# Spectral convolution and normalized residual: the second pass stores 16 map rows, the final pass loads eight of them twice

## The chip, the cores and the metric

The kernel runs on one core of one Trainium2 chip. The metric is the device time of one execution in microseconds (us). Before the change it is 3526.03 us, the median of three runs (3515.51 to 3526.76).

## The reference

The input is x, 16 images of 64 channels of 256 x 256 float32 (16.8 MB an image). Two residual layers follow each other:

```
x = x + spectral(_gn(x)) + bias          # rfft2, 32 x 17 modes mixed within 4 heads of 16 channels, irfft2
m  = mean(xf, axis=0);  mu = m / sqrt(max(m0*m0 - sum(m[1:]**2), EPS))     # xf: tokens x channels of _gn(x)
alpha = max(xf[:,0]*mu[0] - xf[:,1:] @ mu[1:], 1 + EPS);  d = arccosh(alpha)
var  = mean(d*d);  coef = d / sqrt(alpha*alpha - 1)
v  = coef*(xf - alpha*mu);  vo = v - v0/(1+mu0) * (mu with 1 added to mu0)
s  = gamma*vo[:,1:]/(sqrt(var)+EPS) + beta;  t = sqrt(1 + sum(s*s))
x = x + [t, s]
```

`_gn` normalizes pairs of channels of an image. The statistics of the second layer need the whole output of the first, and the variance needs alpha of every token, so x is read three times.

## The kernel before

The kernel is three blocks that follow each other, each with a program for every engine (SP issues most DMAs, GpSimd and ScalarE some). Times are from the start of the profiled span.

**stage_a** (0 to about 1030 us) reads x, computes the 32 x 17 modes, mixes them and stores a spectrum (`spec`) and statistics for every image. The change does not touch it.

**stage_b** (to about 1927 us) is the second pass. It reads an image as 8 tiles of 128 x 4096 (2 MB each, four buffers; SP's `load` of a tile waits until TensorE has finished the tile four before it). Per image:

- GpSimd's `load_modes(b)` asks for the image's spectrum `spt` (two DMAs), `load_dense` for channel 0 (`x0d`).
- VectorE's `combine(b)` contracts the spectrum with the weights of the image (L846 to L853) and raises `v_ready`.
- TensorE's `contract` runs over the 8 tiles; after tile 5 comes `layer_rows(b)` (needs `combine(b)`), after tile 6 `layer_cols(b)`, which needs ScalarE's `copy_z(b)` (L738, L739).
- VectorE's `dense(b)` (L868 to L897), once TensorE has finished the image, makes the maps: `coef` and `beta`, each split into three bf16 parts (high, middle, low), with ScalarE's `distances(b)` (L743 to L751) in between.
- The parts go to DRAM as `maps`, 24 rows of bf16 an image: each part is stored as two rows for the two halves of a channel (s = 0, 1), and each such pair is stored **twice** (index g of `maps_v`). GpSimd's `store_dense` writes the copy g = 0 (L801), along with `bmap` (L802) and `dmap` (L803). ScalarE's `repeat_maps` writes the copy g = 1 (L759, L760), three DMAs for each quarter of the partitions, twelve in all.

The order in each engine's queue is that of its `entry`. On VectorE it is combine(b), dense(b-1), combine(b+1), dense(b). On GpSimd, `entry(b)` is

```
load_modes(b)          # spectrum of b, after combine(b-1)
store_urows(b - 1)
load_dense(b)          # waits for x10 of dense(b-1)
store_dense(b - 1)     # waits for the end of dense(b-1)
```

so the request for the spectrum of b+1 stands behind the stores of image b-1. On ScalarE it is copy_z(b), distances(b), repeat_maps(b), and repeat_maps waits for the end of dense(b), with copy_z(b+1) behind it.

**stage_c** (to the end) is the final pass: 16 tiles of 128 x 2048 an image, four buffers for loads and four for results (`ot`, part of keep_x). For each tile SP issues, in this order, `load_maps` (L1071: 24 rows of 4 KB into every fifth partition of `rt`, then L1073: two DMAs of `bmap`, two partitions each), `load_x` (L1063, 1 MB) and `store` (L1079, 1 MB) of the tile four before the one whose maps are asked for. TensorE multiplies the map rows of `rt` by `lw` (L1160, `p_f` and `p_p`) and the inverse transform by the modes (L1148, `p_u`), VectorE adds and scales (L1270, L1280), ScalarE shifts and squares (L1225, L1232), GpSimd adds (L1322). Rows of `rt` that hold no map are zero. Which row of `lw` meets which part of the split weights is set by masks in `constants()`; six products of parts stand for one float32 product, so a part is needed in one, two or three of them. With 12 rows for each of coef and beta, each product has rows of its own.

Of the kernel before, what the change touches and what calls it, by code (L numbers as in the profile page):

```python
# [19 lines left out]
BF16 = mybir.dt.bfloat16  # L20
ALU = mybir.AluOpType
# [5 lines left out]
HALF = N // 2  # L27
# [7 lines left out]
MAP_AT, MAP_STEP = 4, 5  # L35
MAP_PAIRS = ((0, 2, 4), (1, 3), (5,))


def constants():
# [38 lines left out]
    m = np.zeros((128, 24))  # L78
# [7 lines left out]
    for a, at in enumerate((12, 18)):  # L86
        for part, pairs in enumerate(MAP_PAIRS):
            for pair in pairs:
                for s in range(2):
                    m[MAP_AT + MAP_STEP * (12 * a + 2 * pair + s), at + 2 * part + s] = 1.0  # L90
# [485 lines left out]
def stage_b(nc, ctx, io, B, keep):  # L576
# [7 lines left out]
    maps_v = io["maps"].rearrange("b (q g s) (k j n) -> b g j (s k) q n", q=6, g=2, j=4, n=512)  # L584
# [9 lines left out]
    again_out = sem("again_out")  # L594
# [5 lines left out]
    with ExitStack() as mem:  # L600
# [26 lines left out]
        maps = sb("maps", [128, 6, 512], BF16)  # L627
# [103 lines left out]
        def _(act):  # L731
# [21 lines left out]
            def repeat_maps(b):  # L753

                act.wait_ge(maps_ready, b + 1)
                for j in range(4):
                    at = slice(32 * j, 32 * j + 32)
                    for a in (0, 3):
                        act.dma_start(maps_v[b, 1, j, :, a:a + 2], maps[at, a:a + 2]).then_inc(again_out, 16)  # L759
                    act.dma_start(maps_v[b, 1, j, :, 2::3], maps[at, 0::3]).then_inc(again_out, 16)  # L760

            def entry(b):
                copy_z(b)
                distances(b)
                repeat_maps(b)
# [5 lines left out]
            act.wait_ge(again_out, B * 192)  # L771

        @block.gpsimd
        def _(pool):
# [22 lines left out]
            def store_dense(b):  # L797
                pool.wait_ge(maps_ready, b + 1)
                for j in range(4):
                    at = slice(32 * j, 32 * j + 32)  # L800
                    pool.dma_start(maps_v[b, 0, j], maps[at]).then_inc(maps_out, 16)  # L801
                    pool.dma_start(dense_v(io["bmap"])[b, j], beta[at]).then_inc(beta_out, 16)  # L802
                pool.dma_start(io["dmap"][b], dmap[:].rearrange("p m n -> p (m n)")).then_inc(dmap_out, 16)  # L803

            def entry(b):
                load_modes(b)
                store_urows(b - 1)
                load_dense(b)
                store_dense(b - 1)
# [9 lines left out]
            for b in range(2):  # L819
                P.tensor_copy(awc[:, b, :, 15:47:16], aw[:, b]).then_inc(w_ready[b], 2)  # L820
            load_dense(0)
            pool.wait_ge(uw_ready, 1)
            entry(1)
            with pool.Fori(2, B) as b:
                entry(b)
            store_urows(B - 1)
# [9 lines left out]
        def _(dve):  # L836
# [22 lines left out]
            def dense(b, par):  # L859
# [3 lines left out]
                if not is_at(b, 0):  # L863
                    dve.wait_ge(dmap_out, b * 16)
                    dve.wait_ge(beta_out, b * 64)
                    dve.wait_ge(maps_out, b * 64)
                    dve.wait_ge(again_out, b * 192)
# [17 lines left out]
                both = ((coef, 0, w1), (beta, 3, w2))  # L885
# [10 lines left out]
                ch.inc(V.tensor_tensor(maps[:, 2], w1[:], maps[:, 1], ALU.subtract))  # L896
                V.tensor_tensor(maps[:, 5], w2[:], maps[:, 4], ALU.subtract).then_inc(maps_ready, 1)  # L897
# [108 lines left out]
PER_B = 15  # L1006
# [8 lines left out]
def stage_c(nc, ctx, io, B, keep):  # L1015
# [21 lines left out]
    with ExitStack() as mem:  # L1037
# [20 lines left out]
        def _(sp):  # L1058
# [6 lines left out]
            def load_maps(b, t):  # L1065
# [5 lines left out]
                sp.dma_start(r[MAP_AT:MAP_AT + 24 * MAP_STEP:MAP_STEP], maps_v[b, t]).then_inc(r_in[t % NB], 16)  # L1071
# [57 lines left out]
        def _(pe):  # L1129
# [7 lines left out]
            def first_layer(b, t, n):  # L1137
                g = b * GR + 2 * t + n
                if n == 0:
                    pe.wait_ge(r_in[t % NB], b * (48 * T // NB) + 48 * (t // NB) + 48)  # L1140
# [207 lines left out]
def program(nc, args, B):  # L1348
    io = dict(args)
    dram = lambda n, s, d=FP32: nc.dram_tensor(n, s, d, kind="Internal").ap()  # L1350
    with ExitStack() as ctx:
# [4 lines left out]
        io["maps"] = dram("maps", (B, 24, HALF), BF16)  # L1356
# [52 lines left out]
```

## Time and profile before

| | before |
|---|---|
| median of 3 runs | 3526.03 us (3515.51 to 3526.76) |
| the profiled execution: time, span | 3532.95 us, 3531.4 us |
| busy: TensorE, VectorE, ScalarE, GpSimd | 82%, 75%, 61%, 43% of the span |
| moved by DMA | 1211.86 MB, 343 GB/s on average |
| DMA packets | 289224 |
| of them on ScalarE's queue (q10), 192 issues | 15360, 12.60 MB |
| granted TensorE clock, mean | 0.91 |

The three stages have different limits, so the totals say little; the stages have to be read one by one. The share of DMA time in a stretch is a mean over 16 DMA engines: at 1.00 all sixteen are busy all the time. "Idle before <-releaser" is the time in which an engine had nothing to run, and what ended it.

### The profile page before, as it was taken

How to read it: one execution, taken by the hardware profiler on the slowest of the kernel's cores; microseconds unless marked ns; L12 is line 12 of the kernel's file. 1: busy time of each engine (PE TensorE's matmuls, PEld its weight loads, DVE VectorE, ACT ScalarE, POOL GpSimd, SP SyncE). 2: the span in 40 equal slices, each digit the busy share in tenths (PEclk: the TensorE clock that was granted, in tenths of full speed). 3: DMA queues.
4: the chain of work that ended last, by engine and by line, in shares of the span. 5: the costliest groups of instructions: out<-in, count | busy, mean ns of one | idle time of the engine just before them, and what ended most of it. 6: DMA issues, size and time to landing. Idle time of an engine off the chain costs nothing. (4 is left out here: it accounts for less than half of the span.)

```text
span 3531.4 us, 69910 instructions
## 1 busy us (share of the span) xinstructions
PE 2885.8 (82%) x26018; PEld 1417.7 (40%) x26018; DVE 2643.3 (75%) x2594; ACT 2159.8 (61%) x2994; POOL 1521.1 (43%) x895
## 2 busy tenths in 40 slices
PE   6999999999725776676673998888889888888887
PEld 3555555555501222222222544444444444444443
DVE  0788888888878544644643898888888888888888
ACT  6988888888600101101101788877778778777777
POOL 0101010101111112112111787777778777777777
PEclk9999999999858978888886999999999999999999
DMA  9888787879629999999995899999999999999998
GB/s 376 299 306 301 290 312 279 324 275 327 263 82 357 361 391 398 398 378 378 385 378 185 310 376 391 377 369 385 381 379 373 372 375 370 372 371 379 378 383 341
DMA packets 289224, 1211.86 MB, mean 343 GB/s; under 512 B 32305, under 2 KB 45302, under 8 KB 206710
## 3 DMA queue, kind: packets, MB, share of 16 engines
q1 hardware_dynamic: 258518, 1152.93, 85.1%
q0 software_dynamic: 15136, 43.40, 3.8%
q10 hardware_dynamic: 15360, 12.60, 1.2%
q8 instruction: 148, 2.42, 0.3%
q14 instruction: 62, 0.51, 0.0%
HBM read 884.40 MB, written 324.32 MB: 342 GB/s over the span
## 5 line engine op out<-in xcount | busy, mean ns | idle before, releaser
L1322 POOL TENSOR_TENSOR keep_x<-keep_x,c_pp 128x1024 f32<-128x1024 f32 x512 | 1215.3, 2375 | 360.1 <-DVE keep_x L1280 358.9
L1270 DVE SCALAR_TENSOR_TENSOR keep_x<-keep_x,keep_k,c_p_u 128x1024 f32<-128x1024 f32 x512 | 653.8, 1277 | 126.5 <-PE c_p_u L1148 100.1
L1280 DVE SCALAR_TENSOR_TENSOR keep_x<-c_p_f,keep_k,keep_x 128x1024 f32<-128x1024 f32 x512 | 657.2, 1284 | 107.5 <-DMA out<-keep_x 57.3
L1225 ACT ACTIVATE c_pp<-c_p_p,keep_cols 128x1024 f32<-128x1024 f32 x512 | 571.2, 1116 | 254.8 <-PE c_p_p L1160 253.5
L1148 PE MATMUL c_p_u<-keep_mv,c_zc 64*128 64x256 f32 x4096 | 594.1, 409 | 75.7 <-DVE keep_x L1270 74.6
L1232 ACT ACTIVATE c_sq<-keep_x,keep_cols 128x1024 f32<-128x1024 f32 x512 | 584.8, 1142 | 61.0 <-DVE keep_x L1270 60.7
L336 ACT ACTIVATE a_junk<-keep_x 128x1024 bf16<-128x1024 f32 x512 | 537.9, 1055 | 27.2 <-DMA keep_x<-in_x 19.9
L255 PE MATMUL a_p_rows<-keep_x,a_dft_h 128*64 128x512 f32 x2048 | 514.9, 646 | 37.1 <-DMA a_bias_t<-in_bias 18.7
L1148 PEld LDWEIGHTS c_p_u<-keep_mv,c_zc 64*128 64x128 f32 x4096 | 360.6, 190 | 358.5 <-issue 218.2
L1160 PE MATMUL c_p_f<-c_rt,keep_lw 64*128 64x512 bf16 x1024 | 313.2, 386 | 103.7 <-DVE keep_x L1280 91.1
L522 POOL TENSOR_TENSOR a_sm<-a_sm 128x8 f32<-128x8 f32 x16 | 26.8, 1674 | 824.8 <-DVE a_sm L463 824.8
L685 PE MATMUL b_p_al<-keep_x,b_awc 128*32 128x512 f32 x2048 | 288.9, 640 | 89.7 <-DMA keep_x<-in_x 64.2
L743 ACT ACTIVATE b_dn<-b_dn,b_minus 128x512 f32<-128x512 f32 x16 | 11.6, 724 | 500.5 <-DVE b_dn L871 500.5
L1160 PE MATMUL c_p_p<-c_rt,keep_lw 64*128 64x512 bf16 x1024 | 316.4, 390 | 0.0
L403 DVE TENSOR_REDUCE a_y<-a_prod 128x68 f32<-128x2176 f32 x128 | 309.9, 2421 | 5.6
L400 DVE TENSOR_TENSOR a_prod<-a_wm,a_xh 128x2176 f32<-128x2176 f32 x128 | 309.3, 2416 | 0.3
L1174 PE MATMUL c_p_t<-c_sq,c_hw 128*32 128x512 f32 x2048 | 288.5, 637 | 1.3 <-ACT c_sq L1232 1.3
L846 DVE TENSOR_TENSOR b_prod<-b_spt,b_arow 64x2176 f32<-64x2176 f32 x16 | 38.7, 2417 | 333.9 <-DMA b_spt<-spec 333.8
L685 PE MATMUL b_p_ls<-keep_x,b_awc 128*32 128x512 f32 x2048 | 280.3, 622 | 0.0
L1134 PEld LDWEIGHTS c_p_z<-keep_idft,keep_ys 128*37 128x37 f32 x7936 | 232.5, 114 | 105.6 <-issue 105.6
L1134 PE MATMUL c_p_z<-keep_idft,keep_ys 128*37 128x64 f32 x7936 | 271.6, 221 | 0.0
L255 PEld LDWEIGHTS a_p_rows<-keep_x,a_dft_h 128*64 128x64 f32 x2048 | 136.1, 146 | 308.2 <-issue 187.2
(205 smaller groups left out, 3007.2 us busy)
## 6 DMA issues: line engine op xcount, KB each, us to landing
keep_x<-in_x SPq DMA_DIRECT2D x512, 1024.0 KB, 12.3
keep_x<-in_x SPq DMA_DIRECT2D x128, 2048.0 KB, 16.4
out<-keep_x SPq DMA_DIRECT2D x256, 1024.0 KB, 16.2
c_rt<-maps SPq DMA_DIRECT2D x256, 96.0 KB
maps<-b_maps ACTq DMA_DIRECT2D x192, 64.0 KB, 13.1
maps<-b_maps POOLq DMA_DIRECT2D x64, 192.0 KB, 9.2
dmap<-b_dmap POOLq DMA_DIRECT2D x16, 768.0 KB, 13.8
c_dmap<-dmap SPq DMA_DIRECT2D x16, 768.0 KB, 16.3
```

The source lines that it names most:

```text
L255: last = nc.tensor.matmul(p_rows[i][64 * t:64 * t + 64, :], dft_h[:, j], xt[q % NX][:, t::2, i, j * W:(j + 1) * W], start=(j == 0), stop=( ...
L336: nc.scalar.activation(junk[h % 2][:].rearrange("p (i w) -> p i w", i=2), xt[q % NX][:, h], ACT.Square, accum_out=sq[:, q, h:h + 1]).then_ ...
L403: ch.step(V.tensor_reduce(y[:, 2 * q:2 * q + 2, 0:M2].rearrange("p o (a k) -> p o a k", a=2), prod[:].rearrange("p o a (k n) -> p o a k n" ...
L685: last = nc.tensor.matmul(out[32 * j:32 * j + 32, :], awc[:, par, kind, 15 - k:47 - k], xt[t % NX][:, at:at + 512], start=(k == 0), stop=F ...
L1134: last = nc.tensor.matmul(p_z[64 * at:64 * at + YS, 64 * c:64 * c + 64], ys[:, 8 * part + c], idft[:, chunk, at], start=True, stop=True)
L1148: last = nc.tensor.matmul(p_u[:, 512 * at + W * r:512 * at + W * r + W], zc[t // CH][64 * at:64 * at + 64, i], mv[t % NB][64 * at:64 * at ...
L1160: last = nc.tensor.matmul(p[:, 512 * k:512 * k + 512], keep["lw"][at:at + 64, b].rearrange("p c s -> p (c s)"), rt[t % NB][at:at + 64, c:c ...
L1225: S.activation(pp[n][:], p_p[:], ACT.Identity, bias=keep["cols"][:, b, 1:2]).then_inc(pp_done, 1)
L1232: S.activation(sq[t % 2][:, 1024 * n:1024 * n + 1024], xt[t % NB][:, 1024 * n:1024 * n + 1024], ACT.Square, scale=keep["cols"][:, b, 0:1]) ...
L1270: V.scalar_tensor_tensor(out=u, in0=u, scalar=kc, in1=p_u[:], op0=ALU.mult, op1=ALU.add).then_inc(u_done, 1)
L1280: V.scalar_tensor_tensor(out=ot[t % NB][:, at], in0=p_f[:], scalar=kinv, in1=xt[t % NB][:, at], op0=ALU.add, op1=ALU.mult).then_inc(f_done, 1)
L1322: P.tensor_tensor(o, o, pp[n][:], ALU.add).then_inc(o_done, 1)
```

## The change

Each part is stored once. `maps` becomes 16 rows an image: eight that the final pass needs twice or once in an order fixed by `MAP_ROWS`. VectorE writes eight bf16 maps in place of six: 0 to 3 as before (coef high and middle, beta high and middle), 4 and 6 are copies of 0 and 2 (one instruction over both), 5 and 7 are the low parts. GpSimd's DMA L801 of 32 x 6 x 512 becomes one of 32 x 8 x 512. `repeat_maps` goes from ScalarE, with its wait and its twelve DMAs an image, and so does VectorE's wait for them.

In the final pass `load_maps` issues two DMAs for the maps in place of one: rows 0 to 7 of the 16, each read into two partitions (16 partitions, every eighth from 2), and rows 8 to 15 (8 partitions, every sixteenth from 6). Together they fill 24 partitions as before.

GpSimd's `entry(b)` asks for the spectrum of b+1 first, so the request stands behind combine(b) and in front of load_dense(b) and store_dense(b-1).

```diff
-MAP_AT, MAP_STEP = 4, 5
-MAP_PAIRS = ((0, 2, 4), (1, 3), (5,))
+TWICE_AT, ONCE_AT = 2, 6
+MAP_ROWS = (((0, 0), (0, 1), (1, 1)), ((2, 0), (2, 1)), ((1, 0),))
...
-        maps = sb("maps", [128, 6, 512], BF16)
+        maps = sb("maps", [128, 8, 512], BF16)
...
-            def repeat_maps(b):
-
-                act.wait_ge(maps_ready, b + 1)
-                for j in range(4):
-                    at = slice(32 * j, 32 * j + 32)
-                    for a in (0, 3):
-                        act.dma_start(maps_v[b, 1, j, :, a:a + 2], maps[at, a:a + 2]).then_inc(again_out, 16)
-                    act.dma_start(maps_v[b, 1, j, :, 2::3], maps[at, 0::3]).then_inc(again_out, 16)
-
             def entry(b):
                 copy_z(b)
                 distances(b)
-                repeat_maps(b)
...
-                    pool.dma_start(maps_v[b, 0, j], maps[at]).then_inc(maps_out, 16)
+                    pool.dma_start(maps_v[b, j], maps[at]).then_inc(maps_out, 16)
...
-            def entry(b):
-                load_modes(b)
-                store_urows(b - 1)
+            def entry(b, last=False):
+                if not last:
+                    load_modes(b + 1)
+                store_urows(b)
                 load_dense(b)
                 store_dense(b - 1)
...
+            load_modes(1)
             load_dense(0)
             pool.wait_ge(uw_ready, 1)
+            store_urows(0)
             entry(1)
...
-                    dve.wait_ge(again_out, b * 192)
...
-                both = ((coef, 0, w1), (beta, 3, w2))
+                both = ((coef, 0, w1), (beta, 2, w2))
...
-                ch.inc(V.tensor_tensor(maps[:, 2], w1[:], maps[:, 1], ALU.subtract))
-                V.tensor_tensor(maps[:, 5], w2[:], maps[:, 4], ALU.subtract).then_inc(maps_ready, 1)
+                ch.inc(V.tensor_copy(maps[:, 4::2], maps[:, 0:4:2]))
+                ch.inc(V.tensor_tensor(maps[:, 5], w1[:], maps[:, 1], ALU.subtract))
+                V.tensor_tensor(maps[:, 7], w2[:], maps[:, 3], ALU.subtract).then_inc(maps_ready, 1)
...
-                sp.dma_start(r[MAP_AT:MAP_AT + 24 * MAP_STEP:MAP_STEP], maps_v[b, t]).then_inc(r_in[t % NB], 16)
+                sp.dma_start(r[TWICE_AT::8], maps_v[b, t, 0:8].unsqueeze(1).to_broadcast((8, 2, TC))).then_inc(r_in[t % NB], 16)
+                sp.dma_start(r[ONCE_AT::16], maps_v[b, t, 8:16]).then_inc(r_in[t % NB], 16)
...
-        io["maps"] = dram("maps", (B, 24, HALF), BF16)
+        io["maps"] = dram("maps", (B, 16, HALF), BF16)
```

GpSimd's queue in the second pass, before the change: `entry(1)`, which is written out ahead of the loop (L781 is load_modes, L788 store_urows, L795 load_dense, L801 to L803 store_dense).

```order
L781 DMA b_spt<-spec 32x4x592 x2
L788 DMA spec<-b_uw 8x16x3
L795 DMA b_dn<-in_x 32x512 x4
L801 DMA maps<-b_maps 32x6x512
L802 DMA bmap<-b_dn 32x512
...
L803 DMA dmap<-b_dmap 128x1536
```

The same place after the change: the first two rows of spectrum, dense input and urows are those that stand ahead of `entry(1)`, which begins with the second L770 (L770 is load_modes, L777 store_urows, L784 load_dense, L790 to L792 store_dense).

```order
L770 DMA b_spt<-spec 32x4x592 x2
L784 DMA b_dn<-in_x 32x512 x4
L777 DMA spec<-b_uw 8x16x3
L770 DMA b_spt<-spec 32x4x592 x2
L777 DMA spec<-b_uw 8x16x3
L784 DMA b_dn<-in_x 32x512 x4
L790 DMA maps<-b_maps 32x8x512
L791 DMA bmap<-b_dn 32x512
...
L792 DMA dmap<-b_dmap 128x1536
```

The spectrum requests moved one image ahead, and the map stores are four DMAs of eight maps in place of six.

SP's queue in the final pass, before: the maps, bmap, x and the store of one tile.

```order
L1071 DMA c_rt<-maps 24x2048
L1073 DMA keep_mv<-bmap 2x2x512 x2
L1063 DMA keep_x<-in_x 128x2048
L1079 DMA out<-keep_x 128x2048
L1071 DMA c_rt<-maps 24x2048
```

And after:

```order
L1063 DMA c_rt<-maps 16x1x2048
L1064 DMA c_rt<-maps 8x2048
L1066 DMA keep_mv<-bmap 2x2x512 x2
L1055 DMA keep_x<-in_x 128x2048
L1072 DMA out<-keep_x 128x2048
```

One DMA of 24 rows became one of 16 partitions and one of 8; the rest of the tile's order is the same.

## Rows read from the trace of the kernel before

**Rows 1.** Windows: PE, PEld, DVE, ACT, POOL busy (instructions), granted clock, DMA share, GB/s.

```profile
1131.00:1161.00 30.00, 18.51 (x112) 7.29 (x116) 16.71 (x11) 3.15 (x5) 5.62 (x11) 0.64 0.60 184
1160.00:1869.00 709.00, 500.98 (x3736) 163.47 (x3728) 369.93 (x350) 83.36 (x123) 117.94 (x212) 0.85 1.00 387
...
2110.00:3480.00 1370.00, 1211.42 (x14128) 612.43 (x14124) 1174.64 (x942) 1090.33 (x1121) 1066.75 (x458) 0.97 0.97 376
```

**Rows 2.** Timeline of VectorE, one image of the second pass: start, us, line.

```profile
1414.93 2.42 DVE L846 TENSOR_TENSOR b_prod<-b_spt,b_arow 64x2176 f32<-64x2176 f32 x1 [22.56 <-DMA b_spt<-spec]
...
1429.26 0.75 DVE L868 TENSOR_SCALAR b_dn<-b_p_al,b_ac 128x512 f32<-128x512 f32 x1 [0.67 <-PE b_p_ls L685]
...
1443.12 0.69 DVE L897 TENSOR_TENSOR b_maps<-b_dn,b_maps 128x512 bf16<-128x512 f32 x1
...
1466.85 2.42 DVE L846 TENSOR_TENSOR b_prod<-b_spt,b_arow 64x2176 f32<-64x2176 f32 x1 [22.63 <-DMA b_spt<-spec]
```

**Rows 3.** Timeline of GpSimd, the same image.

```profile
1444.54 0.59 POOL L801 DMA_DIRECT2D maps<-b_maps  x1 [10.95 <-DVE b_maps L897]
...
1450.48 1.20 POOL L781 DMA_DIRECT2D b_spt<-spec  x2 [0.44 <-issue]
```

**Rows 4.** Timeline of ScalarE, then of TensorE, one image earlier.

```profile
1392.14 0.80 ACTq L759 DMA_DIRECT2D maps<-b_maps  x2
...
1398.21 0.59 ACT L738 ACTIVATE b_zs<-b_p_z 34x512 f32<-34x512 f32 x1 [12.97 <-issue]
...
1399.12 2.07 PE L704 MATMUL b_p_y<-keep_idft_w,b_zs 34*128 34x256 f32 x4 [12.10 <-ACT b_zs L739]
```

**Rows 5.** Timeline of TensorE, the second image of the second pass.

```profile
1142.49 2.07 PE L704 MATMUL b_p_y<-keep_idft_w,b_zs 34*128 34x256 f32 x4 [26.36 <-ACT b_zs L739]
```

**Rows 6.** Timeline of TensorE in the last image of the second pass, then of VectorE.

```profile
1852.46 1.07 PE L685 MATMUL b_p_al<-keep_x,b_awc 128*32 128x512 f32 x8 [1.24 <-DMA keep_x<-in_x]
1857.35 1.06 PE L685 MATMUL b_p_al<-keep_x,b_awc 128*32 128x512 f32 x8 [1.25 <-DMA keep_x<-in_x]
1860.92 1.05 PE L695 MATMUL b_p_z<-keep_idft_h,b_vm 128*34 128x256 f32 x4
...
1879.08 2.07 PE L704 MATMUL b_p_y<-keep_idft_w,b_zs 34*128 34x256 f32 x4 [13.10 <-ACT b_zs L739]
...
1886.20 1.93 PE L685 MATMUL b_p_ls<-keep_x,b_awc 128*32 128x512 f32 x8
...
1893.08 0.75 DVE L868 TENSOR_SCALAR b_dn<-b_p_al,b_ac 128x512 f32<-128x512 f32 x1 [21.42 <-DMA maps<-b_maps]
```

**Rows 7.** DMA queues (packets, MB, share of 16 engines) and issues, 1160 to 1880 us.

```profile
q0 software_dynamic: 11256, 35.80, 14.6%
q10 hardware_dynamic: 12686, 10.41, 4.8%
...
maps<-b_maps ACTq DMA_DIRECT2D x168, 64.0 KB, 13.7
maps<-b_maps POOLq DMA_DIRECT2D x56, 192.0 KB, 9.5
```

**Rows 8.** DMA, 1932.4 to 1933.9 us: one tile's maps and bmap.

```profile
DMA packets 48, 0.11 MB, mean 77 GB/s; under 512 B 16, under 2 KB 16, under 8 KB 48
...
q1 hardware_dynamic: 48, 0.11, 26.1%
```

**Rows 9.** Timelines of the final pass: VectorE's first tile; SP, one tile.

```profile
1952.18 1.28 DVE L1270 SCALAR_TENSOR_TENSOR keep_x<-keep_x,keep_k,c_p_u 128x1024 f32<-128x1024 f32 x1 [21.36 <-PE c_p_u L1148]
...
2262.08 0.75 SPq L1071 DMA_DIRECT2D c_rt<-maps  x1
...
2266.44 0.37 SPq L1079 DMA_DIRECT2D out<-keep_x  x1
```

**Rows 10.** Waits of VectorE, 2110 to 3480 us: total, times, longest.

```profile
DVE keep_x L1280 <- DMA out<-keep_x: 56.4, 87, 1.5
DVE keep_x L1270 <- DMA keep_x<-in_x: 21.5, 29, 1.4
```

**Rows 11.** Timeline of GpSimd and ScalarE: the last stores of the second pass.

```profile
1912.17 0.57 POOL L803 DMA_DIRECT2D dmap<-b_dmap  x1
...
1919.07 0.32 ACTq L760 DMA_DIRECT2D maps<-b_maps  x1
```

More of the change, by code:

```diff
@@ L86, in constants @@
     for a, at in enumerate((12, 18)):
-        for part, pairs in enumerate(MAP_PAIRS):
-            for pair in pairs:
+        for part, rows in enumerate(MAP_ROWS):
+            for kind, n in rows:
                 for s in range(2):
-                    m[MAP_AT + MAP_STEP * (12 * a + 2 * pair + s), at + 2 * part + s] = 1.0
+                    row = ONCE_AT + 16 * (4 * a + 2 * n + s) if kind == 1 else TWICE_AT + 8 * (2 * (4 * a + 2 * n + s) + kind // 2)
+                    m[row, at + 2 * part + s] = 1.0
     c["misc"] = m
@@ L583, in stage_b @@
     dense_v = lambda a: a.rearrange("b s (k j n) -> b j (s k) n", j=4, n=512)
-    maps_v = io["maps"].rearrange("b (q g s) (k j n) -> b g j (s k) q n", q=6, g=2, j=4, n=512)
+    maps_v = io["maps"].rearrange("b (q s) (k j n) -> b j (s k) q n", s=2, j=4, n=512)
     x_in, bc_in = keep["bx_in"], keep["bc_in"]
@@ L593, in stage_b @@
     e_ready, maps_ready, maps_out, beta_out, dmap_out = sem("e_ready"), sem("maps_ready"), sem("maps_out"), sem("beta_out"), sem("dmap_out")
-    again_out = sem("again_out")
     var_in, var_mm, std_ready = sem("var_in"), sem("var_mm"), sem("std_ready")
@@ L770, in _ @@
                 entry(b)
-            act.wait_ge(again_out, B * 192)
         @block.gpsimd
@@ L820, in _ @@
                 P.tensor_copy(awc[:, b, :, 15:47:16], aw[:, b]).then_inc(w_ready[b], 2)
+            load_modes(1)
             load_dense(0)
             pool.wait_ge(uw_ready, 1)
+            store_urows(0)
             entry(1)
-            with pool.Fori(2, B) as b:
+            with pool.Fori(2, B - 1) as b:
                 entry(b)
-            store_urows(B - 1)
+            entry(B - 1, last=True)
             store_dense(B - 1)
@@ L1003, in _ @@
             ch.step(V.tensor_scalar(keep["k"][:, 2:3], keep["k"][:, 0:1], 2.0, None, ALU.mult))
-PER_B = 15
+PER_B = 16
 def load_modes_0(sp, keep, spec, half):
@@ L1139, in first_layer @@
                 if n == 0:
-                    pe.wait_ge(r_in[t % NB], b * (48 * T // NB) + 48 * (t // NB) + 48)
+                    pe.wait_ge(r_in[t % NB], b * (64 * T // NB) + 64 * (t // NB) + 64)
                     if t % CH == 0:
```

## The prediction

> **What bounds the kernel now.** I read the windows by stage first, then the timelines of one image of the second pass, engine by engine, and last the DMA queues. The first pass (to about 1030 us) is not touched, so it drops out.
>
> In the second pass the sixteen DMA engines are full: share 1.00 at 387 GB/s from 1160 to 1869 us [rows 1]. Next to that stands a loop of waits of the same length. VectorE ends an image's maps at 1443.8 (L897) and then waits 22.63 us for the next spectrum [rows 2]. GpSimd issues the stores first, from 1444.54, and asks for the spectrum at 1450.48 [rows 3]; it is there at 1466.85. Combine (1414.93 to about 1428.6) and dense (1429.26 to 1443.8) follow. From L846 to L846 that is 1466.85 - 1414.93 = 51.9 us, all of it accounted for: 6 us of GpSimd's issues, 16.4 us of landing, 13.7 us of combine, 15.2 us of dense, and small waits.
>
> The second thing to see is TensorE. ScalarE copies the rows that TensorE needs (L738) only after its own stores, which wait for the end of dense: stores from 1392.14, the copy at 1398.21, TensorE at 1399.12 after 12.10 us of waiting [rows 4]. In mid-stage the four tile buffers cover this, since the DMA share is still 1.00. At two places they don't. In the second image the same wait is 26.36 us [rows 5], and the DMA share between 1131 and 1161 us falls to 0.60 [rows 1]: 0.40 x 30 = 12 us of DMA lost. In the last image nothing is left to hide it: tiles reach TensorE 4.9 us apart (1852.46, 1857.35), the wait is 13.10 us, and the matmuls after it run at the lower clock (1.93 us for eight, against 1.06 before it), so that dense starts at 1893.08 [rows 6].
>
> In the final pass the DMA share is 0.97, TensorE is busy 1211 and VectorE 1175 of 1370 us [rows 1], and VectorE waits in turn for stored buffers (56.4 us) and loads (21.5 us) [rows 10]. I take DMA as its limit, and a few of the sixteen engines, not their mean. One tile's maps and bmap are 24 packets of 4 KB and eight of 2 KB, 32 in all, plus 16 small ones that close a DMA on each engine it uses [rows 8]; 16 = 12 + 2 + 2, so 24 rows go over 12 engines with two rows each, and each bmap DMA over two. If all start from the same engine, the busiest carries per tile 65.5 KB of loads, 65.5 of stores, 8.2 of maps, 8.2 of bmap and 6.5 for its part of dmap, spectrum and channel 0 (1.65 MB an image over 16 engines and 16 tiles): 154 KB. A tile takes (3531 - 1952)/256 = 6.17 us [rows 9], so this engine moves 25.0 GB/s. An engine of the second pass at share 1.00 moves 387/16 = 24.2 GB/s. The mean engine of the final pass moves 376/16 = 23.5. So the busiest is already at full pace.
>
> **The second pass, part by part.** *Twelve DMAs of ScalarE go.* q10 is 4.8% of 720 us, 34.6 us of all sixteen engines for 168 issues, 14 images [rows 7]: 2.47 us an image. *GpSimd's stores grow* from 12 to 16 rows, 0.262 MB an image. q0 takes 14.6% of 720 us for 35.80 MB [rows 7], 2.94 us per MB, so +0.77 us. Net 1.70 us an image; for the 15 images whose stores fall under the loads, -25.5 us. *ScalarE's wait goes*, and with it the loss at the start: -12 us. *The spectrum is asked for after combine instead of behind the stores.* This opens the loop: during dense (15.2 us) the 16.4 us of landing are nearly over, so VectorE's 22.6 us shrink to one or two. By itself this gives nothing, as the DMA engines are at 1.00; it only keeps the loop from being the limit at 51.9 once the DMA work is 50.2. What is late next is the load of x. TensorE has 3.57 us of work a tile (1857.35 to 1860.92 [rows 6]) against some 6.2, so it is not. One thing moves the other way: dense of the last image but one now ends before the last tile has been read, where its stores came after it. These are 2.10 MB of q0: 2.94 x 2.10 = +6.2 us. The last tile thus lands 25.5 + 12 - 6.2 = 31 us sooner.
>
> *The end of the pass.* The last tile came two tiles after the one at 1857.35, by 1868 to 1869. Without the 13.10 us, and with the clock up, dense could start 3.6 us later, at 1872.6, against 1893.08: -20 us. Its own stores end no later: GpSimd's last issue was at 1912.17, ScalarE's at 1919.07 [rows 11]; I count -1. Second pass: -31 - 20 - 1 = -52 us. The bounds: -35, if the start's loss stays as waits of another kind and late stores cost what they save; -65, if the engines, freed of ScalarE's 1 KB packets, also run the x loads better.
>
> *Costed at nothing:* VectorE's added copy of two maps. All of dense is 15.2 us and VectorE idles 22.6 an image [rows 2]; were that cover gone, it would be under 1 us an image. load_dense(0) now waits behind combine(0), long before dense(0). In the final pass SP issues one DMA more a tile: an issue takes 0.75 us, and SP's tile runs from 2262.08 to 2266.4 of some 6 [rows 9].
>
> **The final pass.** The bytes and the 24 filled partitions are the same, but one DMA of 24 rows becomes one of 8 rows read twice and one of 8. I take the twice-read DMA to be cut where both of its sides can be cut, at the 8 rows in memory, as 24 rows were cut into 12 x 2 [rows 8]. Then eight engines carry 2 + 1 = 3 rows where twelve carried 2, and the busiest gets one 4 KB row more per tile. At 25.0 GB/s that is 4.1/25.0 = 0.164 us, times 256 tiles: **+42 us**. The low end is 0: the busiest engine carries two rows as before, or the mean decides. For the high end the isolated tile of rows 8 serves: 26.1% of 16 engines over 1.5 us is 6.3 us for 115 KB, 0.22 us for 4.1 KB, so +57. I stay near the low price, since in the full queue a row is one packet among long ones.
>
> The Trainium skill (DMA: Bandwidth & Descriptors, "Why a DMA increments its semaphore by 16 and not by 1") speaks against this change: a DMA issued from SP runs on the largest number of engines up to 16 that divides the slowest dimension of both patterns, the lowest-numbered ones. The 12 and 2 of this trace agree; for 16 partitions against 8 rows it gives 8, beginning with the same engines as bmap, and thus the sum above. The same page's rules for kernel authors say that DMAs of all issuers share the same 16 engines, so that leaving ScalarE's queue is no loss; the rows show shares by queue, not that.
>
> **The sum.** -52 + 42 = -10 us. The profiled execution took 3532.95, so its like would take 3523. It stood 7 us above the median of the three runs; from that median the forecast is **3516 us**. The bound between a change and none is 0.3%, 10.6 us, so the forecast sits just inside it: the two halves are each five times larger than their difference.
>
> **The rivals.**
>
> 1. *The final pass loses nothing.* The DMA of 16 partitions uses 16 engines, so that the busiest has 1 + 1 rows, or the mean share of 0.97 is what counts, and that does not change. For it: VectorE's DMA waits are only 78 us of 1370 [rows 10], and the busy shares of TensorE and VectorE are close behind [rows 1]. Against it: 0.97 is what is left if most engines idle while a few are full; if 154 KB is the pace and the mean is 145, 0.94 would be expected. Then 3526 - 52 = 3474 us. Chance 0.17.
> 2. *The third row costs more than its bytes* (the other side). The second maps DMA is short and lands rows in the middle of long loads on the same eight engines; at the price of rows 8, 0.22 us a tile, the final pass loses 57, and with 38 us of gain in the second pass the kernel ends at 3545 us, slower. It decides from 52/256 = 0.20 us a tile upwards. For it: three DMAs on the same first engines. Against: full-queue rates are near the low price. Chance 0.16.
> 3. *The second pass gains only bytes.* Its DMA engines are full now, and the start's 12 us come back as a wait for loads, or the spectrum (which is asked for only after combine, late in the image) stays exposed. Then 25.5 - 6.2 + 20 = 39 us against 42: 3529 us. Chance 0.15.
>
> **How the numbers follow.** The main case has 0.52 and by itself the range 3505 to 3527; it gives faster and same in about equal parts (0.27, 0.24, 0.01). Rival 1 is faster, rival 3 the same, rival 2 slower, with small parts over the edges: faster 0.45, same 0.38, slower 0.17. The range reaches nearly to rival 1's time and takes in most of rival 2's: 3478 to 3541 us.
>
> **What would show it.** Right: VectorE's wait for b_spt is a few us an image; TensorE's wait for b_zs is gone; the distance of L846 to L846 is near 50 us; dense of the last image starts about 50 us sooner; the share from 1131 on shows no hole; the final pass, from its first L1148 to the end, is some 40 us longer, its DMA share falls below 0.97, and a tile's maps close with 8 + 8 + 2 + 2 = 20 small packets. Wrong: 28 small packets with an unchanged final pass (rival 1); a final pass longer by 55 (rival 2); an image still at 52 us (rival 3). If the share stays at 0.97 while the pass grows, my busiest engine is not the cause.

## The result and the profile after

| | before | after |
|---|---|---|
| median | 3523.59 us (16 runs, 3512.08 to 3548.53, and one of 10876.57) | 3546.37 us (16 runs, 3529.41 to 3562.65) |
| ratio | | 1.0062, 95% interval 1.0042 to 1.0082 |
| profiled execution: time, span | 3532.95, 3531.4 us | 3538.95, 3537.4 us |
| granted TensorE clock, mean | 0.910 | 0.924 |

The kernel became slower by 22 us, where 10 us faster was forecast. The profile of before lay 9 us above its median and that of after lies 7 us below its own, so that two spans side by side hide most of the difference. Times between kernels are therefore taken from ratios to the kernel before (on the same chip each time) and turned into microseconds with 3524.

The page of the profile after: its span, its packets and its two large queues. The third queue of before (q10, ScalarE's) has no line any more.

```profile
span 3537.4 us, 69577 instructions
...
DMA packets 275915, 1203.49 MB, mean 340 GB/s; under 512 B 30257, under 2 KB 30966, under 8 KB 193398
...
q1 hardware_dynamic: 259542, 1152.93, 86.5%
q0 software_dynamic: 16160, 47.60, 3.8%
```

The windows of after, which answer to [rows 1] (the last one lies 50 us earlier, as the final pass does):

```profile
1131.00:1161.00 30.00, 23.31 (x184) 5.66 (x176) 12.86 (x5) 0.00 (x0) 6.12 (x11) 0.90 1.01 412
1160.00:1820.00 660.00, 479.51 (x3498) 142.35 (x3498) 380.34 (x373) 83.54 (x123) 118.54 (x211) 0.91 1.01 384
2060.00:3430.00 1370.00, 1181.14 (x13698) 600.04 (x13695) 1132.01 (x908) 1054.84 (x1083) 1030.39 (x442) 0.96 0.96 365
```

The hole at the start of the second pass is filled (DMA share 0.60 before, 1.01 now), and the pass stays full. In the final pass the share fell from 0.97 to 0.96 and the rate from 376 to 365 GB/s: the same work moves more slowly, by engines that are hardly less busy.

The second pass of after, where [rows 2 to 4] and [rows 6] were. VectorE (end of dense, then combine), one image:

```profile
1405.76 0.68 DVE L889 TENSOR_TENSOR b_maps<-b_dn,b_maps 128x512 bf16<-128x512 f32 x1
1406.67 0.17 DVE L895 COPY b_awc<-b_aw 128x4 f32 x1 [0.23 <-DVE b_maps L889]
1407.19 2.42 DVE L838 TENSOR_TENSOR b_prod<-b_spt,b_arow 64x2176 f32<-64x2176 f32 x1 [0.34 <-issue]
```

GpSimd's request, and TensorE behind ScalarE's copy:

```profile
1390.92 1.20 POOL L770 DMA_DIRECT2D b_spt<-spec  x2 [24.82 <-DVE b_vm L845]
```

```profile
1383.26 1.13 PE L704 MATMUL b_p_y<-keep_idft_w,b_zs 34*128 34x256 f32 x4
```

The request goes out as soon as combine ends, the spectrum is there when VectorE wants it (0.34 us in place of 22.63), and the 12 us of TensorE have gone too. From the first L838 of an image to that of the next, images 3 to 14 take 48.9 us on average, where the same images took 53.7 before (the 51.9 of [rows 2] is one of them). The last image, TensorE's sixth tile and VectorE's dense, and then VectorE's first tile of the final pass:

```profile
1831.79 1.07 PE L685 MATMUL b_p_al<-keep_x,b_awc 128*32 128x512 f32 x8 [2.29 <-DMA keep_x<-in_x]
```

```profile
1847.85 0.75 DVE L859 TENSOR_SCALAR b_dn<-b_p_al,b_ac 128x512 f32<-128x512 f32 x1 [29.82 <-PE b_p_ls L685]
```

```profile
1903.16 1.28 DVE L1263 SCALAR_TENSOR_TENSOR keep_x<-keep_x,keep_k,c_p_u 128x1024 f32<-128x1024 f32 x1 [21.36 <-PE c_p_u L1141]
```

The sixth tile came 25.6 us sooner (1857.35 before), dense 45.2 us, the final pass 49.0 us [rows 6, 9]. So the second pass did what it should. The final pass, from that instruction to the end of the span, grew from 3531.4 - 1952.18 = 1579.2 to 3537.4 - 1903.16 = 1634.2 us: 55 us. VectorE's waits in it, against [rows 10]:

```profile
DVE keep_x L1273 <- DMA out<-keep_x: 76.5, 113, 2.0
DVE keep_x L1263 <- DMA keep_x<-in_x: 45.1, 38, 3.5
```

Both grew, by 20 and 24 us: loads and stores come later. SP's queue from 1882 to 1892 us holds the maps and bmap of four tiles and nothing else:

```profile
DMA packets 209, 0.48 MB, mean 48 GB/s; under 512 B 80, under 2 KB 80, under 8 KB 208
...
q1 hardware_dynamic: 208, 0.46, 15.7%
```

80 small packets are 20 a tile, 8 + 8 + 2 + 2. The DMA that reads eight rows twice runs on eight engines, which is what the rule of the Trainium skill gives for 16 partitions against 8 rows (DMA: Bandwidth & Descriptors, "Why a DMA increments its semaphore by 16 and not by 1"). The trace agrees with the number of engines by these packets, and 24 rows over twelve engines had closed with 16. It does not say which engines they are.

### The profile page after: what moved, and what is told of

The parts are those of the page before. It is cut to its first block and busy times, and to the rows that moved or that the text cites. A ratio compares the mean times of both kernels' runs of the same rounds, so it can differ in the third digit from the quotient of the medians.

```text
span 3537.4 us, 69577 instructions
## 1 busy us (share of the span) xinstructions
PE 2903.2 (82%) x26018; PEld 1410.9 (40%) x26018; DVE 2647.2 (75%) x2610; ACT 2160.4 (61%) x2994; POOL 1523.9 (43%) x895
## 5 line engine op out<-in xcount | busy, mean ns | idle before, releaser
L1141 PE MATMUL c_p_u<-keep_mv,c_zc 64*128 64x256 f32 x4096 | 603.4, 414 | 99.4 <-DVE keep_x L1263 93.7
L685 PE MATMUL b_p_al<-keep_x,b_awc 128*32 128x512 f32 x2048 | 305.6, 671 | 225.2 <-DMA keep_x<-in_x 199.6
L685 PE MATMUL b_p_ls<-keep_x,b_awc 128*32 128x512 f32 x2048 | 296.9, 653 | 0.0
L738 ACT ACTIVATE b_zs<-b_p_z 34x512 f32<-34x512 f32 x16 | 9.4, 588 | 461.2 <-PE b_p_zl L696 461.2
L281 PE MATMUL a_p_cols<-a_dft_w,a_cols 128*128 128x34 f32 x2048 | 243.9, 275 | 0.0
## 6 DMA issues: line engine op xcount, KB each, us to landing
b_spt<-spec POOLq DMA_DIRECT2D x32, 296.0 KB, 13.7
```

The lines of the kernel that those rows point to most:

```text
L685: last = nc.tensor.matmul(out[32 * j:32 * j + 32, :], awc[:, par, kind, 15 - k:47 - k], xt[t % NX][:, at:at + 512], start=(k == 0), stop=F ...
L1141: last = nc.tensor.matmul(p_u[:, 512 * at + W * r:512 * at + W * r + W], zc[t // CH][64 * at:64 * at + 64, i], mv[t % NB][64 * at:64 * at ...
```

## The experiments

**The theories.** *A*: the final pass goes at the pace of its busiest DMA engines. They carried four 4 KB rows of maps and bmap a tile before (2 rows of maps, 1 of each bmap DMA) and carry five now (2 + 1 of maps, 1 + 1 of bmap), if all these DMAs begin with the same engines. The rivals: the added DMA of each tile, the double read or the new partitions cost, wherever the rows fall (*B*); the early request for the spectrum made the gain of the second pass (*C*); the number of DMAs, the bytes or the mean load of the engines decide, not where the rows fall (*D*, and *B* in the last run). *F* and *G* are about the second pass alone and come up with experiment 10. The paragraph ahead of each result is what was expected before the run. The diffs show the main lines; the ends `.then_inc(...)` and the counts and masks that follow from an edit are left out.

**1. The same loads on sixteen and eight engines.** The 16 stored rows are read once by one DMA and eight of them again by the other, so that nothing is read twice within a DMA. In this kernel some rows meet the other half of the weights: the same work, another output.

```diff
-                sp.dma_start(r[TWICE_AT::8], maps_v[b, t, 0:8].unsqueeze(1).to_broadcast((8, 2, TC)))
-                sp.dma_start(r[ONCE_AT::16], maps_v[b, t, 8:16])
+                sp.dma_start(r[TWICE_AT::8], maps_v[b, t])
+                sp.dma_start(r[ONCE_AT::16], maps_v[b, t, 0:8])
```

> The changed kernel, but in the final pass all 16 map rows are loaded by one DMA into 16 partitions (every eighth from 2) and the eight that are needed twice by a second one (every sixteenth from 6); the masks follow. Same bytes, same number of DMAs, same 24 partitions; only the rows per DMA engine differ: 1 + 1 on eight engines and 1 on the other eight, where the change has 2 + 1 on eight. Theory A (the busiest DMA engine sets the pace of the final pass): the final pass falls back to its length before the change, some 55 us shorter than after it, and the kernel takes about 3475 to 3495 us. Rival B (the second DMA per tile with its issue on SP, the double read or the new partitions cost the time): it stays near 3546 us.

Measured: 3485.69 us, ratio 0.9892 (0.9871 to 0.9912), final pass 1584.2 us. 60 us faster than the change with the same number of DMAs, rows and bytes, and the same second pass. So neither the added DMA nor the partitions nor the bytes explain these 60 us. Where the rows fall is different, and no DMA reads a row twice; experiments 8 and 11 take these two apart.

**2. The kernel before, with its 24 rows cut into 16 and 8.**

```diff
-                sp.dma_start(r[MAP_AT:MAP_AT + 24 * MAP_STEP:MAP_STEP], maps_v[b, t])
+                for lo, n in ((0, 16), (16, 8)):
+                    at = MAP_AT + lo * MAP_STEP
+                    sp.dma_start(r[at:at + n * MAP_STEP:MAP_STEP], maps_v[b, t, lo:lo + n])
```

> The kernel before, with its 24 rows loaded by two DMAs, of 16 and of 8 rows, into the same partitions. One DMA issue more per tile; at most two rows on any engine, as before. Theory A: the same as before within 0.3% (3513 to 3535 us), closing packets 16 + 8 + 2 + 2 = 28 a tile. Rival B (one more DMA per tile is what costs): 40 to 60 us slower, about 3570 us.

Measured: 3534.52 us (12 runs), ratio 1.0039 (1.0014 to 1.0064), final pass 1591.8 us. The busiest engine has four rows as before; one more DMA a tile costs 14 us (5 to 23), not the 40 to 60 of B. This was a term that the prediction had at nothing.

**3. The change without GpSimd's new order.**

```diff
-            def entry(b, last=False):
-                if not last:
-                    load_modes(b + 1)
-                store_urows(b)
+            def entry(b):
+                load_modes(b)
+                store_urows(b - 1)
```

> The changed kernel with GpSimd's old order: the next spectrum is asked for behind the stores of the dense part. Theory A, by which the second pass gains by bytes, by the DMA hole at its start and by the wait at its end: the loop of waits is back (VectorE waits some 22 us an image for the spectrum), but it is as long as the DMA work, so this is 0 to 20 us slower than the change. Rival C (the early request made the gain of the second pass): 40 us or more slower than the change, about 3590 us.

Measured: 3751.78 us, ratio 1.0657 (1.0630 to 1.0685). A expected 0 to 20 us more than the change, C 40 us or more and a kernel of about 3590 us; it is 210 us. The final pass is as long as in the change (1630.9 us); the second pass ends 216 us later. VectorE's combine of two images, and GpSimd's request between them:

```profile
1428.86 2.42 DVE L835 TENSOR_TENSOR b_prod<-b_spt,b_arow 64x2176 f32<-64x2176 f32 x1 [39.59 <-DMA b_spt<-spec]
...
1496.17 2.42 DVE L835 TENSOR_TENSOR b_prod<-b_spt,b_arow 64x2176 f32<-64x2176 f32 x1 [37.90 <-DMA b_spt<-spec]
```

```profile
1464.53 1.21 POOL L770 DMA_DIRECT2D b_spt<-spec  x2 [0.44 <-issue]
```

An image takes 67.3 us in place of 51.9, and the spectrum lands 31.6 us after its request in place of 16.4. TensorE, and the DMA share of the stretch before the request and of that behind it:

```profile
1442.51 1.91 PE L695 MATMUL b_p_z<-keep_idft_h,b_vm 128*34 128x256 f32 x4 [28.27 <-DVE b_vm L842]
```

```profile
1430.00:1460.00 30.00, 15.93 (x90) 5.75 (x94) 26.84 (x27) 6.02 (x9) 3.29 (x7) 0.65 0.39 147
1464.00:1496.00 32.00, 18.32 (x153) 4.58 (x144) 0.00 (x0) 0.00 (x0) 2.11 (x4) 0.88 1.02 377
```

TensorE stands with all its buffers full while it waits for combine, and the DMA engines idle (0.39). Then it runs through its tiles, the loads of x go out one after another, and the request for the spectrum joins them.

**4. The kernel before, with GpSimd's new order alone.** The reverse of that diff.

> The kernel before with GpSimd's new order alone; ScalarE still stores its 12 rows an image. Theory A: ScalarE's wait in front of its copy for TensorE stays whenever dense ends late, but dense now starts as soon as TensorE has finished an image, so the copy comes early and TensorE's waits of 12 us an image shrink as well; the DMA work is unchanged at some 51 us an image; gain 5 to 35 us, 3490 to 3520 us. Rival C: the whole 50 us of the second pass, 3475 us.

Measured: 3514.14 us (12 runs), ratio 0.9971 (0.9952 to 0.9989): 10 us faster (4 to 17), as A had it and far from C's 3475. With ScalarE's wait in place the order matters little.

**5. Two DMAs of twelve rows.** Two of the eight stored maps are copies, so the high parts of coef and beta are in fact stored twice and only the other parts once. The stored rows are put in another order (the copies are now maps 0 and 6), so that two overlapping DMAs, rows 0 to 11 and rows 4 to 15, fill the 24 partitions.

```diff
-                sp.dma_start(r[TWICE_AT::8], maps_v[b, t, 0:8].unsqueeze(1).to_broadcast((8, 2, TC)))
-                sp.dma_start(r[ONCE_AT::16], maps_v[b, t, 8:16])
+                for at, lo in ((FIRST_AT, 0), (SECOND_AT, 4)):
+                    sp.dma_start(r[at:at + 12 * ROW_STEP - ROW_STEP + 1:ROW_STEP], maps_v[b, t, lo:lo + 12])
```

> The changed kernel with the 16 stored rows in another order and two loads of 12 rows each that overlap (rows 0 to 11 and 4 to 15), so each of twelve DMA engines gets one row from each: two rows on the busiest, as before the change, and the reference's result. Theory A (the busiest engine sets the pace): as the 16 + 8 form, 3480 to 3495 us, some 60 us under the change. Rival B (the new partitions or the double read cost the time, and the 16 + 8 form was quick for another reason): above 3520 us.

Measured: 3489.99 us, ratio 0.9910 (0.9884 to 0.9936), final pass 1590.7 us. It leaves nothing out and is faster than both kernels: 54 us less than the change (42 to 66), 32 us less than before. VectorE's two waits fall back to those of [rows 10]:

```profile
DVE keep_x L1273 <- DMA out<-keep_x: 56.0, 90, 1.8
DVE keep_x L1263 <- DMA keep_x<-in_x: 25.1, 27, 1.6
```

**6. That kernel without bmap**, which it loads for the first four tiles only; the term of beta in the other tiles is left out.

```diff
-                    sp.dma_start(m[64 * at + M2:64 * at + M2 + 2]..., bmap_v[b, t, at])
+                    if b == 0 and t < NB:
+                        sp.dma_start(m[64 * at + M2:64 * at + M2 + 2]..., bmap_v[b, t, at])
```

> The same, but bmap is loaded for the first four tiles only, and each later tile uses what lies in its buffer; the beta term of the other tiles is left out of the right place, so this measures the cost of those two small DMAs of a tile, 8 KB on each of two engines. Theory A: these two engines lose 8 KB of about 154 a tile and no longer stand out against the ten others with two map rows: 50 to 85 us faster than the form with bmap, about 3420 us, until compute (5.54 us a tile where no DMA is waited for) takes over. Rival D (the mean of the engines or HBM is the limit): 16 KB of 2.3 MB a tile, 0.7% of 1600 us, at most 12 us faster.

Measured: 3418.66 us, ratio 0.9708 (0.9685 to 0.9732), 71 us less. By D these 16 KB of a tile are worth 12 us at most. The two DMAs are 28 us of the 71 by the price of experiment 2, the rest falls to two rows on two engines. Two rows at 54 us (the step from experiment 5 to the change) and two DMAs would be some 135 us; but ten other engines now have two rows as well, and VectorE's waits for stores, 56 us in experiment 5, are 3.6. What limits this kernel was not looked for further.

**7. The change with one more DMA of two rows**, one more row on two engines.

```diff
+                sp.dma_start(spare[t % NB][:], maps_v[b, t, 0:2]).then_inc(r_in[t % NB], 16)
```

> The changed kernel with one more DMA per tile, of two rows of 4 KB into a spare tile that nobody reads: one row more on two engines. Theory A: the busiest engines carry four rows, +42 us for the row and about +12 for the DMA itself (the 16 + 8 form of the kernel before cost 11): 3590 to 3610 us. Rival D: 8 KB of 2.3 MB, +5 us, plus 12 for the DMA: 3560 us.

Measured: 3628.65 us, ratio 1.0313 (1.0281 to 1.0345), 88 us more than the change. Less 14 us for a DMA that is 74 us for a row. It is above A's 3590 to 3610 and further from D's 3560: the price of a row was too low here as well.

**8. The kernel before, its 24 rows in three DMAs of eight**, so that each of eight engines has three.

```diff
-                sp.dma_start(r[MAP_AT:MAP_AT + 24 * MAP_STEP:MAP_STEP], maps_v[b, t])
+                for lo in (0, 8, 16):
+                    at = MAP_AT + lo * MAP_STEP
+                    sp.dma_start(r[at:at + 8 * MAP_STEP:MAP_STEP], maps_v[b, t, lo:lo + 8])
```

> The kernel before with its 24 rows loaded by three DMAs of eight rows into the same partitions: three rows on eight engines, no row read twice. Theory A: +42 us for the third row and about +11 for each of the two added DMAs: 3580 to 3595 us. Rival B (double read or partitions): only the two DMAs, 3540 to 3550 us.

Measured: 3602.80 us, ratio 1.0239 (1.0206 to 1.0271), 70 us more than experiment 2: 14 us for a DMA and 56 us for a row. It is again a little above A's 3580 to 3595, and B's 3540 to 3550 is out. So the price holds in a kernel with the second pass of before, with no row read twice.

**9. bmap by four DMAs of one partition.** Meant to spread bmap over many engines, on the kernel of experiment 5; bmap lies in DRAM such that each of these rows is 4 KB in one piece.

```diff
-                    sp.dma_start(m[64 * at + M2:64 * at + M2 + 2]..., bmap_v[b, t, at])
+                    for s in range(2):
+                        p = 64 * at + M2 + s
+                        sp.dma_start(m[p:p + 1].rearrange("p (e n) -> p e n", e=PIECES), bmap_v[b, t, at, s:s + 1])
```

> The kernel with two DMAs of 12 rows, with bmap laid out in DRAM so that each row of a tile is 4 KB in one piece, and loaded by four DMAs of one partition each in place of two DMAs of two partitions. The bytes are the same; two DMAs a tile are added; a DMA of one partition can be cut along its row over many engines. Theory A (the first engines, which carry the most rows, set the pace of the final pass): each of the two bmap DMAs with two partitions put one row on each of two engines, so two rows a tile leave the busiest; at 0.22 us a row that is up to 0.44 x 256 = 113 us less, against two added DMAs at 0.045 us each a tile (+23 us) and more, smaller packets: 3400 to 3470 us against 3490. Theory D (the number of DMAs and of packets sets the pace, not where the rows fall): 3513 us or more.

Measured: 3626.84 us, ratio 1.0314 (1.0298 to 1.0330), 142 us more than experiment 5. By the words on record that speaks for D, but their premise, that such a DMA is cut over many engines, was wrong. SP's queue with the loads of four tiles and nothing else, of experiment 5 (1880 to 1892 us) and then of this one (1881 to 1894 us):

```profile
DMA packets 241, 0.48 MB, mean 40 GB/s; under 512 B 112, under 2 KB 112, under 8 KB 240
...
c_rt<-maps SPq DMA_DIRECT2D x8, 48.0 KB
keep_mv<-bmap SPq DMA_DIRECT2D x8, 8.0 KB
```

```profile
DMA packets 225, 0.48 MB, mean 37 GB/s; under 512 B 112, under 2 KB 112, under 8 KB 224
...
c_rt<-maps SPq DMA_DIRECT2D x8, 48.0 KB
keep_mv<-bmap SPq DMA_DIRECT2D x16, 4.0 KB
```

Both close with 112 small packets, 28 a tile: 12 + 12 + 2 + 2 there and 12 + 12 + 4 x 1 here. Each of the four DMAs ran on a single engine, in one 4 KB packet. If that is the same engine each time, which the trace does not show, the busiest now has 1 + 1 + 4 = 6 rows in place of 4. Two rows at 54 us and two DMAs at 14 are 136 us; 142 were measured. D would have to explain 142 us by two DMAs without a byte more, ten times what one DMA cost in experiment 2. This run was explained after its result, so it supports A less than experiments 5, 8 and 11 do.

**10. Experiment 3 with ScalarE's wait put back**, with no DMA behind it.

```diff
             def entry(b):
                 copy_z(b)
                 distances(b)
+                act.wait_ge(maps_ready, b + 1)
```

> The changed kernel with GpSimd's order of before, as in the run that took 3751.8 us, and ScalarE waits after distances(b) until dense(b) has ended, as repeat_maps made it wait before, but with no DMA behind the wait. Theory F (ScalarE's wait held TensorE's buffers back while the spectrum was on its way, so that no deep queue of x loads stood in front of it; with the wait gone the spectrum lands 15 us later, and that is in the loop): the wait brings the period of an image back from 67 us to about 50 to 52, the spectrum lands in 16 to 20 us, and the time is 3540 to 3600 us. Theory G (what is lost without the new order has another cause, such as the larger stores of GpSimd ahead of the request): the time stays above 3700 us.

Measured: 3562.41 us (4 runs), ratio 1.0130 (1.0112 to 1.0147). One added wait makes the kernel 186 us faster. GpSimd asks at 1444.64 and VectorE goes on at 1458.33:

```profile
1444.64 1.20 POOL L771 DMA_DIRECT2D b_spt<-spec  x2 [0.44 <-issue]
```

```profile
1458.33 2.42 DVE L836 TENSOR_TENSOR b_prod<-b_spt,b_arow 64x2176 f32<-64x2176 f32 x1 [19.96 <-DMA b_spt<-spec]
```

13.7 us in place of 31.6. SP's queue, which holds the loads of x, while the spectrum was under way, in experiment 3 (1464.5 to 1496.2 us) and here (1444.6 to 1458.4 us):

```profile
q1 hardware_dynamic: 649, 9.58, 81.4%
```

```profile
q1 hardware_dynamic: 121, 1.72, 43.3%
```

9.58 MB of x shared the engines with it there and 1.72 MB here, while GpSimd's own queue moved about the same (2.34 and 2.52 MB). An image takes 51.4 us on average (images 3 to 14), against 66.4 in experiment 3. Theory F holds and G is out: the wait that looked like pure loss had held TensorE's buffers back while the spectrum was under way.

**11. Every row read twice.** The rows in the order of experiment 5, one DMA into 32 partitions; eight of them meet weights of zero.

```diff
+                sp.dma_start(r[ROW_AT::ROW_STEP], maps_v[b, t].unsqueeze(1).to_broadcast((16, 2, TC)))
```

> The changed kernel with the 16 stored rows in the order of the kernel with two DMAs of 12 rows, and in the final pass one DMA that reads each of the 16 rows into two partitions (32 partitions, every fourth from 2; the eight that no product needs meet weights of zero). Per tile eight rows (32.8 KB) more are moved than in the changed kernel, by three DMAs in place of four. Theory A (the final pass goes at the pace of its busiest engines): the maps DMA is cut over sixteen engines with two rows each, the busiest has 2 + 2 rows and three DMAs, as in the kernel before; the added rows fall on engines that have time. Against the kernel with two DMAs of 12 rows one DMA a tile goes (-11 us): 3475 to 3485 us, a final pass of about 1579 us, a ratio near 0.988. Theory B (the mean load of the sixteen engines sets the pace): 32.8 KB at 387 GB/s is 0.085 us a tile, +22 us on the changed kernel's rows, so 3500 to 3515 us and a final pass of 1600 us or more.

Measured: 3489.25 us, ratio 0.9904 (0.9882 to 0.9926), final pass 3486.1 - 1901.31 = 1584.8 us. Its windows, against the last row of after above:

```profile
2060.00:3430.00 1370.00, 1213.34 (x14106) 614.49 (x14108) 1172.36 (x941) 1087.96 (x1119) 1065.34 (x456) 0.97 0.99 381
```

It moves 32.8 KB a tile more than the change and takes 56 us less. The share rose to 0.99, so the added bytes are not free: A's 3475 to 3485 was a little low, D's 3500 and more too high (B in the text on record). The DMA that it saves against experiment 5 and the bytes that it adds about cancel. Here every row is read twice within one DMA, and the pass is short: the double read is not what costs in the change.

**The runs in one table** (rows of 4 KB a tile on the busiest engine, DMAs a tile for maps and bmap):

| kernel | rows | DMAs | final pass, profile | ratio |
|---|---|---|---|---|
| before | 4 | 3 | 1579.2 | 1 |
| 4: before, new order | 4 | 3 | 1578.8 | 0.9971 |
| 2: before, 16 + 8 | 4 | 4 | 1591.8 | 1.0039 |
| 8: before, 3 x 8 | 5 | 5 | 1658.9 | 1.0239 |
| 11: all twice | 4 | 3 | 1584.8 | 0.9904 |
| 5: two of twelve | 4 | 4 | 1590.7 | 0.9910 |
| 6: without bmap | 2 | 2 | 1516.4 | 0.9708 |
| 1: sixteen and eight | 4 | 4 | 1584.2 | 0.9892 |
| **after** | 5 | 4 | 1634.2 | 1.0062 |
| 3: after, old order | 5 | 4 | 1630.9 | 1.0657 |
| 10: after, old order, ScalarE waits | 5 | 4 | 1635.0 | 1.0130 |
| 7: after, one row more | 6 | 5 | 1730.8 | 1.0313 |
| 9: bmap by single rows | 6 | 6 | 1719.4 | 1.0314 |

The final pass follows the first two columns, in both families, whatever the second pass was. Experiments 7 and 9 alone stand the other way round, by 11 us of their single profiles; their ratios are equal.

**What the packets say.** The runs show that the placing of a tile's rows sets the time. They do not show the engines beyond the first ones standing idle for it, as one would expect if these alone held the pass up. The stretch from 2060 to 3430 us of before, of experiment 8 and of experiment 7:

```profile
2060.00:3430.00 1370.00, 1215.46 (x14224) 614.76 (x14224) 1176.15 (x942) 1096.56 (x1128) 1071.35 (x459) 0.97 0.98 376
2060.00:3430.00 1370.00, 1166.51 (x13566) 591.59 (x13564) 1120.43 (x900) 1045.59 (x1075) 1022.58 (x438) 0.97 0.98 359
2060.00:3430.00 1370.00, 1126.83 (x12936) 568.47 (x12940) 1072.79 (x862) 998.11 (x1023) 973.44 (x417) 0.95 0.96 345
```

In experiment 8 the DMA share is that of before, at 359 in place of 376 GB/s. Added up over the packets of the final pass in the traces, as a mean of the sixteen engines:

| kernel | final pass | in packets | idle | mean of an 8 KB packet |
|---|---|---|---|---|
| 6 | 1516.4 us | 1489.7 us | 26.7 us | 329 ns |
| before | 1579.2 us | 1523.6 us | 55.6 us | 334 ns |
| 5 | 1590.7 us | 1534.8 us | 56.0 us | 337 ns |
| 2 | 1591.8 us | 1536.1 us | 55.7 us | 337 ns |
| after | 1634.2 us | 1550.3 us | 83.9 us | 341 ns |
| 8 | 1658.9 us | 1595.2 us | 63.7 us | 351 ns |
| 7 | 1730.8 us | 1632.1 us | 98.7 us | 359 ns |

The 8 KB packets are the rows of x and of the result, some 64,900 in each kernel, and their median is 309 ns in every one. Of the 55 us between before and after, half is idle time and half is longer packets; from experiment 2 to 8, and from after to 7, it is nearly all longer packets. Why the packets of x take longer when the first engines carry one row more is not shown by any run.

## Why the prediction was wrong

Three differences lead from before to after: experiment 2, experiment 5 and the change.

| step | forecast | measured, from ratios |
|---|---|---|
| one more DMA a tile (2 against before) | 0 | +14 (5 to 23) |
| second pass (5 against 2) | -52 | -45 (-58 to -33) |
| third row on eight engines (after against 5) | +42 | +54 (42 to 66) |
| sum | -10 | +22 (rounded once) |

- **The step that failed** is the price of the final pass, "4.1/25.0 = 0.164 us, times 256 tiles: +42 us", with the added DMA of each tile "costed at nothing". Together they measured 14 + 54 = 68 us, 0.27 us a tile. The placing was right: the twice-read DMA runs on eight engines (20 small packets a tile), so that they have three rows, and the first engines are shared with bmap as far as experiment 6 shows it. The row is 0.21 us a tile here and 0.22 in experiment 8, the high end that came from the isolated tile [rows 8], and 0.29 in experiment 7. The argument for the low end, that in a full queue a row is one packet among long ones, was not borne out for the pass, though it was for the packet: a 4 KB packet took 159 ns (median of 2110 to 3400 us) before and after, which is the 0.164 of the sum. What the sum lacks is what the row does to the packets around it. On the added DMA the prediction looked only at SP's time to issue it; whether its 14 us lie there or on the engines is open.
- **The second pass** came within its bounds. From the sixth tile of the last image on: -25.6 us where -31 was forecast, then -19.6 to dense (forecast -20) and -3.8 to the final pass (forecast -1); these are differences of two profiles, of which that of before was slower than its median (see below). The start's hole is gone, as forecast. Experiment 10 splits it: against the change it still has the old order and ScalarE's wait, and is 24 us slower (15 to 33). If the parts add up, the remaining 21 us of 45 are ScalarE's DMAs less GpSimd's larger stores, where the sum had 25.5, or 19 with the 6.2 of the last stores.
- **"By itself this gives nothing"**, of the early request, was wrong in a way that no rival had. Alone in the kernel before it gives 10 us; but without ScalarE's wait it is what keeps the loop of spectrum, combine and TensorE short, and the kernel without it takes 210 us more. "What is late next is the load of x" was right of the change and wrong of the change without the new order, where the spectrum is late (experiment 3).
- **Rival 2** is what happened, by a slightly other sum: 57 against 38 us there, 68 against 45 here. Its deciding point was 52/256 = 0.20 us a tile; the final pass lost 0.27. Rival 1 is out (20 small packets, a longer final pass). Rival 3 is out by its signs: the start has no hole (share 1.01), VectorE's wait for the spectrum is gone, and an image takes 48.9 us. Its gain of 39 us by itself lies within the measured 33 to 58.
- **The last sign** of the prediction reads against it: "If the share stays at 0.97 while the pass grows, my busiest engine is not the cause." The share went to 0.96, where the prediction's way of counting (145 KB on the mean engine, 158 on the busiest) would have it at 0.92, and in experiment 8 it did not fall at all. Experiments 1, 5, 8 and 11 show that the rows on the busiest engines decide; that they do so by leaving the other engines idle is only half true of the change and hardly of experiment 8.
- The base was off as well. The profile of before was slower than its median: its final pass began at 1952.2 us, while those of experiments 2 and 8, with the same first two passes, began at 1929.1 and 1942.8. The seven profiles with the second pass of after began it between 1897.9 and 1903.2.

## What to carry to other kernels

Where DMA bounds a stage, count rows and DMAs on the busiest engine, not the mean: the small closing packets of an isolated tile tell how many engines each DMA takes, and a row a tile moved off the busiest engines was worth 54 us here while eight rows added by a DMA over all sixteen cost no more than the one DMA saved with them. Price an added row from a stretch where it stands alone, not by its bytes at the full queue's rate, and never price an added DMA at zero. A DMA share that hardly moves does not clear the engines: the packets may have grown longer instead. Before a wait is taken out, ask which loads it was holding back: two edits that belong together have to be costed together, since one of them alone cost 210 us here.

## What the runs showed of the hardware that was not expected

- A DMA of one partition with 4 KB in one piece went out as one packet on one engine (experiment 9: four closing packets for four DMAs), though both of its sides were written as eight pieces.
- A request of 0.6 MB (two DMAs of 296 KB) landed 13.7 us after it was issued in experiment 10 and 31.6 us in experiment 3, with the DMA share at 1.00 and 1.02. Both times the engines were full; the difference lay in what filled them, 43% and 81% of it SP's loads of x.
- A short DMA of one 4 KB row on each of two engines, plus the wait for it, costs 88 us over 256 tiles, 0.34 us each (experiment 7), where 4.1 KB at the 24 GB/s of an engine would be 0.17 us.
- One more 4 KB row a tile on eight engines, with one more DMA, left the median of the 8 KB packets at 309 ns and raised their mean from 337 to 351 ns (experiment 8 against 2), with the DMA share at 0.98 in both from 2060 to 3430 us.
